# Attention inside an adaLN block: query preparation further ahead, two table and spread buffers, block order 3, 1, 2, 0

## What is computed

```python
q = _rms_norm(x @ w_qa, q_a_norm_w) @ w_qb
q_nope, q_rope = (q[..., :D_NOPE], q[..., D_NOPE:])
...
q_rope = _apply_rope(q_rope, cos, sin)
k_rope = _apply_rope(k_rope[:, None], cos, sin)
...
scores = jnp.einsum('bhsd,bhtd->bhst', q_full, k_full) * scale
scores = jnp.where(mask[None, None], scores, jnp.finfo(scores.dtype).min)
attn = jax.nn.softmax(scores, axis=-1)
out = jnp.einsum('bhst,bhtd->bhsd', attn, v)
```

## Time and profile before

| | |
|---|---|
| median of three runs | 1425.6 us |
| the profiled execution's own time | 1426.01 us |
| its span | 1424.2 us |
| PE busy | 1235.5 us, 87% |
| DVE busy | 948.5 us, 67% |
| ACT busy | 789.6 us, 55% |
| POOL busy | 724.5 us, 51% |
| mean granted TensorE clock | 0.943 of full |
| L658 POOL subtraction, 128x1024 | 192 of 1988 ns |
| L757 DVE addition, 64x512 | 64 of 1447 ns |
| L775 DVE spread, 128x512 | 64 of 1320 ns |
| L783 DVE seed, 128x512, from 170 to 1140 us | 60 of 687 ns |

### The profile page before, as it was taken

How to read it: one execution, slowest core, us unless ns; L and a number is a source line. 1 busy time by engine, 2 the same in 40 slices (tenths; PEclk the granted TensorE clock), 3 DMA queues, 4 the chain that set the end, 5 groups by cost and what they waited for, 6 DMA issues and landing times. The chain is left out here.

```text
span 1424.2 us, 24513 instructions
## 1 busy us (share of the span) xinstructions
PE 1235.5 (87%) x9452; PEld 973.6 (68%) x9452; DVE 948.5 (67%) x1836; ACT 789.6 (55%) x1166; POOL 724.5 (51%) x569
## 2 busy tenths in 40 slices
PE   2756998998899889989988998999899987989897
PEld 2653675776677667757766775776677766878786
DVE  3535667767676576667677766767576767676776
ACT  1251775776567567656766675666577753232232
POOL 0121576577566566665776675676566762111100
PEclk9875999999899999989999999999899988999998
DMA  9201001001000000010010001000100040000000
GB/s 261 67 0 38 16 16 39 1 16 35 19 16 16 24 16 16 16 38 2 16 39 16 16 16 30 10 16 24 30 1 16 16 135 14 1 15 0 15 15 15
DMA packets 57671, 39.54 MB, mean 28 GB/s; under 512 B 7744, under 2 KB 57152, under 8 KB 57408
## 3 DMA queue, kind: packets, MB, share of 16 engines
q1 hardware_dynamic: 51216, 33.94, 8.0%
q10 hardware_dynamic: 6352, 4.19, 1.2%
HBM read 33.66 MB, written 4.46 MB: 27 GB/s over the span
## 5 line engine op out<-in xcount | busy, mean ns | idle before, releaser
L764 DVE TENSOR_REDUCE gates<-bank 128x1 f32<-128x512 f32 (+3 forms) x640 | 382.7, 608 | 230.9 <-PE bank L839 158.1
L658 POOL TENSOR_TENSOR pt_lo<-pt 128x1024 f16<-128x1024 f32 x192 | 381.1, 1988 | 262.2 <-ACT pt L715 262.2
L715 ACT ACTIVATE pt<-pair 128x1024 f32<-128x1024 f32 x192 | 196.2, 1022 | 143.8 <-PE pair L864 142.4
L706 ACT ACTIVATE pair<-shift 128x1024 f32<-128x1024 f32 x256 | 263.3, 1029 | 8.1
L882 PE MATMUL bank<-values,pt 128*128 128x129 f16 x2176 | 241.3, 225 | 0.6 <-DVE rowsum L796 0.6
L664 POOL TENSOR_TENSOR pt_lo<-pt 128x512 f16<-128x512 f32 (+3 forms) x256 | 184.9, 741 | 105.2 <-ACT pt L719 103.8
L882 PEld LDWEIGHTS bank<-values,pt 128*128 128x128 bf16 x2176 | 196.5, 99 | 54.6 <-issue 37.7
L884 PE MATMUL bank<-values,pt_lo 128*128 128x65 f16 x2176 | 229.7, 195 | 0.0
L884 PEld LDWEIGHTS bank<-values,pt_lo 128*128 128x128 f16 x2176 | 197.4, 100 | 0.0
L839 PE MATMUL bank<-kt_a_hi,q_hi 128*128 128x512 f32 (+2 forms) x320 | 137.8, 436 | 54.0 <-ACT q_hi L688 38.1
L719 ACT ACTIVATE pt<-pair 128x512 f32<-128x512 f32 (+3 forms) x256 | 108.6, 434 | 106.9 <-PE pair L867 106.8
(11 more groups left out here) (217 smaller groups left out, 2368.5 us busy)
## 6 DMA issues: line engine op xcount, KB each, us to landing
turn_by<-rope_cos_by_feature SPq DMA_DIRECT2D x64, 128.0 KB, 2.9
turn_by<-rope_sin_by_feature SPq DMA_DIRECT2D x64, 128.0 KB, 3.0
xs<-in_L_attn_x ACTq DMA_DIRECT2D x1, 2048.0 KB, 25.1
lat<-in_L_attn_w_o SPq DMA_DIRECT2D x1, 2048.0 KB, 26.5
xs_again<-in_L_attn_x SPq DMA_DIRECT2D x1, 2048.0 KB, 8.2
out<-xs_again SPq DMA_DIRECT2D x4, 512.0 KB, 2.8
lat<-in_L_wmod SPq DMA_DIRECT2D x1, 1536.0 KB, 15.8
lat<-in_L_attn_w_qb SPq DMA_DIRECT2D x1, 1152.0 KB, 7.8
```

Source lines behind the costliest of these rows:

```text
L658: pool.tensor_tensor(out=pt_lo[:, at].rearrange("p a n -> p (a n)"), in0=full, in1=cut(full), op=ALU.subtract).then_inc(low_ok, 1)
L706: act.activation(s_pair[u % 2][:, :, :], shift[:, item % SHIFTS:item % SHIFTS + 1, :].to_broadcast([P, 2, BW]), ACT.Copy).then_inc(seeded[ ...
L715: act.activation(pt[:, at], s_pair[u % 2][:, :, :], ACT.Exp).then_inc(exp_done, 1)
L764: dve.tensor_reduce(out=mx[:, item % MAXIMA, t, part:part + 1], in_=work_of(w)[:, 0:n * P], axis=AXX, op=ALU.max).then_inc(work_seen["v"], 1)
```

## The change

- The order of the blocks within a head pair becomes 3, 1, 2, 0.
- First query products 6 rounds ahead of the pair's first chunk (before: 4); `item_shift` 5 rounds ahead of an item (before: 4), and with it all chunks one round earlier; shift products 3 ahead (before: 2).
- Three slots for queries instead of four; two buffers for the tables and two for `spread`. SP loads the tables for each pair as soon as `query_sum` of the pair two back is done.
- `spread` is written by four multiplications of the 128x128 identity with one column of `nmx` each.
- Within a round DVE does `item_shift` right after the chunk maxima, ahead of query work and seed.

```diff
-PAIRS = [(hp, g) for hp in range(NP) for g in (3, 2, 1, 0)]
+PAIRS = [(hp, g) for hp in range(NP) for g in (3, 1, 2, 0)]
...
-PT_RING, SHIFTS, Q_SLOTS, MAXIMA = 4, 4, 4, 4
+PT_RING, SHIFTS, Q_SLOTS, MAXIMA = 4, 4, 3, 4
...
-AHEAD = 4
+AHEAD, PREP_AHEAD = 5, 6
...
-SHIFT_ROUND = [FIRST_UNIT[i] - 2 for i in range(NI)]
+SHIFT_ROUND = [FIRST_UNIT[i] - 3 for i in range(NI)]
...
-    PREP_ROUND[_p] = min([CHUNK_ROUND[FIRST_CHUNK[2 * _p]] - 4] + [r - 4 for r in PREP_ROUND[_p + 1:_p + 2]])
+    PREP_ROUND[_p] = min([CHUNK_ROUND[FIRST_CHUNK[2 * _p]] - PREP_AHEAD] + [r - 4 for r in PREP_ROUND[_p + 1:_p + 2]])
...
-        turn_by = sb(own, "turn_by", [P, 2, BW])
+        turn_by = sb(own, "turn_by", [P, 2, 2, BW])
...
-        spread = sb(own, "spread", [P, BT, P], F32R)
+        spread = sb(own, "spread", [P, 2, BT, P], F32R)
...
-                    if g != table_of:
-                        table_of, tables_in = g, tables_in + 1
-                        if p > 0:
-                            sp.wait_ge(q_sum, 2 * p)
-                        for n, name in enumerate(("cos_t", "sin_t")):
...
+                    if p > 1:
+                        sp.wait_ge(q_sum, 2 * p - 2)
+                    for n, name in enumerate(("cos_t", "sin_t")):
...
-                    if item > 0:
-                        dve.wait_ge(work_done, WORK[("shift", item - 1)] + 1)
-                    dve.tensor_tensor(out=spread[:, :, :], in0=ident[:, :].unsqueeze(1).to_broadcast([P, BT, P]),
-                                      in1=nmx[:, item % 2, :].unsqueeze(2).to_broadcast([P, BT, P]),
-                                      op=ALU.mult).then_inc(spread_ok, 1)
+                    if item > 1:
+                        dve.wait_ge(work_done, WORK[("shift", item - 2)] + 1)
+                    for t in range(BT):
+                        dve.tensor_scalar(spread[:, item % 2, t, :], ident[:, :], nmx[:, item % 2, t:t + 1], None,
+                                          ALU.mult).then_inc(spread_ok, 1)
...
                     for c in CHUNKS_AT[r]:
                         maximum(c)
+                    if r in ITEM_MAX_AT:
+                        item_shift(ITEM_MAX_AT[r])
                     p, part = PREP_AT.get(r, (0, 4))
...
-                    if r in ITEM_MAX_AT:
-                        item_shift(ITEM_MAX_AT[r])
```

More of the change, by code:

```diff
@@ L586, in attend @@
         nmx = sb(own, "nmx", [P, 2, BT])
-        spread = sb(own, "spread", [P, BT, P], F32R)
+        spread = sb(own, "spread", [P, 2, BT, P], F32R)
         ones_r = sb(own, "ones_r", [P, P], F32R)
         wq_in = sem("wq_in")
-        turn_in = sem("turn_in")
+        turn_in = [sem(f"turn_in_{n}") for n in range(2)]
         q_sum = sem("q_sum")
@@ L741, in query_turn @@
                             dve.wait_ge(q_lo_ok, 2 * p)
-                        loads = 1 + sum(a[1] != b[1] for a, b in zip(PAIRS[:p], PAIRS[1:p + 1]))
-                        dve.wait_ge(turn_in, 64 * loads)
+                        dve.wait_ge(turn_in[p % 2], 64 * (p // 2 + 1))
                     dve.wait_ge(work_done, n + 1)
@@ L746, in query_turn @@
                         rot = ROT[part]
-                        dve.tensor_tensor(out=qf[rot, part, :], in0=work_of(n)[rot, :], in1=turn_by[rot, 0, :],
+                        dve.tensor_tensor(out=qf[rot, part, :], in0=work_of(n)[rot, :], in1=turn_by[rot, p % 2, 0, :],
                                           op=ALU.mult).then_inc(work_seen["v"], 1)
                     else:
-                        dve.tensor_tensor(out=qs[:, :], in0=work_of(n)[:, :], in1=turn_by[:, 1, :],
+                        dve.tensor_tensor(out=qs[:, :], in0=work_of(n)[:, :], in1=turn_by[:, p % 2, 1, :],
                                           op=ALU.mult).then_inc(work_seen["v"], 1)
```

19 lines of the change are left out of this document (10 added, 9 removed).

## The result

The changed kernel takes **1440.2 us** (median of 4 runs, 1436.9 to 1441.1) against 1426.0 of the kernel before in the same session (4 runs, 1423.8 to 1428.6): a ratio of 1.0095, 95% interval 1.0071 to 1.0119. It is slower by 1%. The forecast was 1389 in a range of 1350 to 1424, with 0.11 on slower: wrong in sign. The profiled execution has a span of 1435.1 us, 10.9 more than before.

The account below looks back on a forecast made before the run. Repeated stalls, not one engine's throughput, were taken to bound the attention: 18.8 us per head pair falling to 13.25, a gain of 5.55. Over seven pairs 38.9, less 1.5, makes 37: 1426 to 1389 us, range 1350 to 1424.

Parts of the forecast that it names:

- I book 1.0 per head pair: Cost of splitting the spread into four multiplications, for a head pair's eight item shifts: 1.0 us.
- rival 4: Split spread pays for everything: POOL gets in twice per spread, 61 us lost, 1450 us; chance 0.11.
- C: Rounds 5 and 6 before, 1 to 3 after: PE's stall for a bank falls from 2.2 to 1.3 us.
- D: Rounds 16 and 17 before, round 9 after, sum alone: PE's stall stays 1.3 us.
- B: Rounds 28 to 31 before, 25 to 27 after: stall falls from 5.0 to 2.1 to 2.2 us.
- I book 0.1 per sum, not 1.2.: Gain from earlier queries: PE would lose its wait for the high part but wait for DVE's maxima instead.
- Rival 1: The lead was worth its waits: sums run 1.4 us instead of 2.99, 35.7 us come free, 1353 us; chance 0.17.
- A: Rounds 25 and 26 before, 21 and 22 after: stall falls from 6.8 to 3.0 us, no DVE wait for tables.
- Rival 2: Tables still late: DVE waits 1 to 2 us for them, seven times, about 1400 us; chance 0.11.
- The start, +1.5: Chunks a round earlier put two more reductions of 0.69 us before the first unit: +1.5 us once.
- The last head pair, unchanged: Seven of eight head pairs prepare a next one and gain; the last, 107.9 us, was forecast to change by 0.
- The stall of 18.8: Per head pair before: 129.0 us against an own pace of 110.2, taken from the last head pair plus query products.

Follow-up runs that it names:

- rounds put back: Changed kernel with scores four rounds ahead instead of five, shifts two instead of three: 1352.2 us with the spread in one product, 1458.1 us with four.
- lead 6, 6 apart: Kernel before with first query products six rounds ahead of the first chunk instead of four, and preparations six rounds apart instead of four: 1344.3 us.

## Why the prediction was wrong

The way from before to after, each step a pair of runs that differ in that edit alone or in the edits named:

| step | time | change |
|---|---|---|
| before | 1426 | |
| lead of six | 1380 | -46 |
| order 3, 1, 2, 0 | 1379 | -1 |
| two tables, two `spread` buffers, three slots, item shift first | 1352 | -27 |
| scores five ahead, shifts three ahead | 1409 | +57 |
| four products | 1440 | +31 |

The step of 27 was not taken further apart; one thing that it ends is DVE's wait for the tables, 27.8 us. The change held a gain of some 74 us, twice what I forecast, and lost 88.

Against the forecast the kernel is 51 us late. The largest part is the term for the split spread: 31 us where 7 were booked. The evacuation's part is smaller in these terms, because waits of nearly its size were booked at the same places for another reason.

1. **"I book 1.0 per head pair" for the split.** Times seven head pairs that is 7 us over the kernel; it cost 31, and 85 to 145 in the other kernels with four products. In the six middle head pairs it cost 2.3 each, and 16.7 at the two ends, of which 1.0 was booked. The mechanism was the forecast's own, not rival 4's: in the changed kernel POOL got in once in rounds 3, 11, 25 and 31 (2.5 us, forecast 2.7 with the maximum), a second time with a short piece in round 33 (3.3), and not at all in the other three (0.87). The price was wrong, on two counts. The one product in this order takes 0.69 us in all rounds but round 3 of a middle head pair, not the 1.57 of before, so that the split adds 1.1 us an item (71.6 us over 64). And what it delays is the evacuation behind it, 1.34 us of PE in round 32, and the seed, 0.89 in round 34, where I had looked at the maxima alone. Rival 4 as it stands, POOL in twice or more, is what the kernels with rounds put back and with the split alone showed. Its objection, that POOL's next operation comes a round later, held in the changed kernel but for round 33; it fails where POOL has a backlog, as after each pair of query low parts.
2. **The places C, D and B, "PE wants that bank".** I followed one consumer of DVE's queue, the work bank, and priced the evacuation as 0.4 us of delay for the maximum behind it. The evacuation has a consumer of its own, and with sums in rounds 1, 9 and 25 that one is the earlier: stalls of 1.88, 1.73 and 3.07 where 1.3, 1.3 and 2.15 were forecast for another wait. (B's own terms, 4.9 + 0.7 + 1.4 + 0.4 + 0.3, add up to 7.7 and not to 7.9.) That the sizes are near is luck. The wait that I forecast was there as well, hidden behind the other: with the evacuation moved ahead it is 1.07, 0.84 and 1.37. What I did not ask at all was what another round would give: one round later, with the evacuation done before the sum, neither wait is there but for 0.64 us in round 28, and the kernel is 57 us faster. Moving the evacuation alone brings back 37. What the other 20 are made of was not taken apart.
3. **"I book 0.1 per sum, not 1.2."** In the changed kernel it was not far off: the sums of rounds 1, 9 and 21 took 2.99 and that of round 25 1.40, as forecast, and behind them PE met DVE again. Rival 1, sums of 1.4, did not come about there. As a statement on the lead it was wrong, and on the low side: the lead alone gave 46 us where the whole forecast was 37. D's 1.3 went entirely (25.35 to 24.01), with a sum of 1.95, and C's too, with a sum that still took 2.99.
4. **A, the stall of 3.0 at the first query product of round 22.** Right: 2.63, with the additions, the seed, the evacuation and the maximum in front of it that I had added up.
5. **The tables, in time when DVE asks.** Right: no wait is left. Rival 2 falls.
6. **What the tables are worth.** By themselves nothing (1425.1); with the lead of six, some part of 35 us. I had put it into A, as part of one sum, which hid that it depends on the lead.
7. **The start, +1.5.** It came to +7.9 up to round 40 where -4.1 was forecast. The first scores start 5.5 us later (4.0 with the spread in one product), and the rest is in the first head pair, which takes 131.2 us, and 124.2 with the spread in one product.
8. **The last head pair, unchanged.** Wrong by 9.7, nearly all of it the split: with the spread in one product it takes 109.3. It prepares no next pair, but it has split spreads like the others, and I counted them only in seven.
9. **The stall of 18.8.** "Nothing else differs between them" is not so. The last head pair also lacks chunk products for a next one, 58 instead of 80. PE's busy time in them, in a head pair of before and in the last:

```profile
662.50:789.10 126.60, 32.31 (x80) 15.40 (x80) 1.00 0.07 20
1046.80:1154.70 107.90, 22.39 (x58) 11.02 (x58) 1.00 0.04 11
```

So part of the 18.8 was work, an estimated 9 us of it: PE busy 114.96 against 103.29 at the same granted clock, less the 2.3 that I had taken for query products. The own pace of 110.2 was too fast. The stretches shown above give, per head pair in us:

| | before | changed | changed, spread in one product | lead 6, 6 apart |
|---|---|---|---|---|
| head pair | 129.0 | 128.25 | 125.9 | 116.1 |
| PE busy | 117.9 | 116.3 | 116.5 | 113.1 |
| PE not busy | 11.2 | 11.9 | 9.4 | 3.0 |

The error stands on both sides of the forecast's sum and did not move 1389. But it hid that the change left PE as idle as before: 11.9 us of 11.2, where the sum took 5.55 off 18.8.

The Trainium skill (SBUF — State Buffer, Who interferes with whom) says that a VectorE instruction with two SBUF inputs also contends with a GpSimd instruction that reads SBUF, and that in a two-port mode whoever issues first has the pair for the whole instruction while the other blocks. I had used the second half for the new form alone. The runs show both forms waiting alike, 5.91 and 6.12 us for four beside POOL.

## What to carry to other kernels

One instruction on DVE beside a busy POOL is worth more than several short ones that add up to the same busy time: price a split by the length of POOL's instructions times the gaps at which it has one ready, not by its own, and ask what stands behind it in the queue. When a table of rounds is shifted, list for every instruction in a queue who waits for its end, not only the one that waited before; one round of shift was worth 57 us here. And measure the parts of a bundled change separately: this one hid a kernel that is 5% faster (1352.2 us) behind two edits that ate it.

## What the runs showed that I had not expected

- Two additions or four products run back to back on DVE let POOL's 1.9 us instructions in between them, the products in either form of instruction, once for each gap at which POOL has one ready; a single product in the same place waits once (1.67 us).
- What a wait is worth can depend on what stands beside it: DVE's 19.3 us for the tables gave nothing when taken away first; taken away behind the lead of six, with one sum moved as well, 25.1 us of it went and the kernel gained 35, a share of which is the moved sum's.
- The granted clock of the attention rose from 0.97 to 1.00 once PE's waits fell to a few us per head pair, and PE's busy time for the same products from 117.9 to 113.1 us per head pair, so part of what a stall costs is paid in the products behind it.
- A stretch that looks like the same work without its stalls may have less work: the last head pair of before had 22 chunk products fewer, and by the estimate above about half of the stall read from it was PE's own work.
